# Values of the local attention projected in 64-column tiles onto both partition halves, copied by one ScalarE instruction in place of four

## The reference

```python
x = attn_layer(shift_tokens(x), Wqkv[i], q_scale[i], k_scale[i], Wo[i]) + x
x = ffn_layer(shift_tokens(x), ln_g[i], ln_b[i], W1[i], b1[i], W2[i], b2[i]) + x
```

## Time and profile before

| | |
|---|---|
| three timed runs | 2869.66, 2869.91 and 2871.89 us, median 2869.91 |
| profiled execution, span on the core | 2876.8 us |
| busy: PE / DVE / ACT / POOL | 2397.0 / 2534.2 / 1993.5 / 1164.0 us |
| value projection, PE L412 | 384 matmul records (two for each instruction), mean 623 ns |
| value copy, ACT L587 | 768 instructions, mean 375 ns, 287.6 us |
| granted TensorE clock, mean | 0.934 of full speed |

### The profile page before, as it was taken

How to read it: one execution, slowest core, us unless ns; L and a number is a source line. 1 busy time by engine, 2 the same in 40 slices (tenths; PEclk the granted TensorE clock), 3 DMA queues, 4 the chain that set the end, 5 groups by cost and what they waited for, 6 DMA issues and landing times. The chain is left out here.

```text
span 2876.8 us, 60131 instructions
## 1 busy us (share of the span) xinstructions
PE 2397.0 (83%) x23276; PEld 1231.6 (43%) x23276; DVE 2534.2 (88%) x2784; ACT 1993.5 (69%) x3169; POOL 1164.0 (40%) x465
## 2 busy tenths in 40 slices
PE   7788898888988889898898888988898765556778
PEld 2344444444444444444444444444444322222256
DVE  5799999899999999999999999999998499999642
ACT  4777787777877778777787777877787563343433
POOL 0344444343444434444444444434443046566220
PEclk8899999999999999999999999999999877777889
DMA  0100000000000000000000000000000100000001
GB/s 26 43 2 2 2 23 9 9 2 2 23 9 9 2 2 23 9 9 2 2 23 9 10 2 2 23 9 10 2 1 1 34 0 0 0 0 0 16 15 44
DMA packets 16015, 29.82 MB, mean 10 GB/s; under 512 B 3616, under 2 KB 6064, under 8 KB 15664
## 3 DMA queue, kind: packets, MB, share of 16 engines
q1 hardware_dynamic: 15760, 25.78, 2.9%
HBM read 24.73 MB, written 1.05 MB: 9 GB/s over the span
## 5 line engine op out<-in xcount | busy, mean ns | idle before, releaser
L697 POOL TENSOR_TENSOR f_rot<-f_raw,f_tabc 128x1024 f32<-128x1024 f32 x192 | 453.2, 2361 | 1070.6 <-DVE f_qk L745 576.5
L701 POOL TENSOR_TENSOR f_rot<-f_rot,f_shuf 128x1024 f32<-128x1024 f32 x192 | 451.5, 2351 | 235.7 <-DVE f_shuf L738 235.7
L738 DVE TENSOR_TENSOR f_shuf<-f_shuf,f_tabs 128x1024 f32<-128x1024 f32 x192 | 420.6, 2191 | 8.7
L596 ACT ACTIVATE f_raw<-f_ps 128x1024 f32<-128x1024 f32 x192 | 196.2, 1022 | 315.6 <-PE f_ps L423 315.6
L770 DVE TENSOR_TENSOR f_s<-f_s,f_rcp 128x512 f32<-128x512 f32 x192 | 400.6, 2087 | 6.6
L422 PE MATMUL f_ps<-f_xs,f_wq 128*128 128x512 f32 x384 | 229.2, 681 | 133.8 <-ACT f_rn L605 95.0
L464 PEld LDWEIGHTS f_ps<-f_ptz,f_v 64*64 64x64 f32 x6144 | 259.9, 133 | 152.3 <-issue 152.3
L1125 POOL TENSOR_TENSOR s_prod<-s_state,s_cs 128x1024 f32<-128x1024 f32 x64 | 234.1, 3676 | 167.3 <-DVE s_state L1203 137.0
L960 PE MATMUL s_ps<-s_prod,s_ident 128*128 128x512 f32 x256 | 182.9, 873 | 133.8 <-POOL s_prod L1125 133.6
L587 ACT ACTIVATE f_v<-f_ps 64x256 f32<-64x256 f32 x768 | 287.6, 375 | 6.6
L464 PE MATMUL f_ps<-f_ptz,f_v 64*64 64x96 f32 (+1 forms) x6144 | 286.2, 243 | 2.2 <-ACT f_ptz L617 2.2
(11 more groups left out here) (263 smaller groups left out, 4035.6 us busy)
## 6 DMA issues: line engine op xcount, KB each, us to landing
e_w<-in_e_w SPq DMA_DIRECT2D x16, 256.0 KB, 2.8
f_wq<-in_f_wq SPq DMA_DIRECT2D x12, 256.0 KB, 2.7
f_wk<-in_f_wk SPq DMA_DIRECT2D x12, 256.0 KB, 3.5
f_wv<-in_f_wv SPq DMA_DIRECT2D x12, 256.0 KB, 3.6
f_wo<-in_f_wo SPq DMA_DIRECT2D x6, 512.0 KB, 3.2
f_w<-in_f_w SPq DMA_DIRECT2D x6, 341.0 KB, 3.0
s_dx<-in_k_pick SPq DMA_DIRECT2D x1, 1536.0 KB, 8.9
f_w<-in_f_w SPq DMA_DIRECT2D x6, 192.0 KB, 3.9
```

What stands on the lines that cost most here:

```text
L697: pool.tensor_tensor(view(rot, 0, [S, 4], [1, S]), view(raw, 0, [S, 4], [1, S]), view(tab_c, 0, [S, 2], [0, 2], [1, S]), ALU.mult).then_in ...
L701: pool.tensor_tensor(rot[:, :], rot[:, :], shuf[:, :], ALU.add).then_inc(sem["rot"], 1)
L738: dve.tensor_tensor(view(shuf, 0, [S, 4], [1, S]), view(shuf, 0, [S, 4], [1, S]), view(tab_s, 0, [S, 2], [0, 2], [1, S]), ALU.mult).then_i ...
```

## The change

`values` computes the same numbers with four products in place of one. Each has 64 tokens (r = 0 or 1) as stationary operand, hence 64 columns of the array, and 256 columns of the weights (four heads of parity h, taken as four runs of 64) as moving operand. Its result lands on partitions 64h to 64h+63, columns 256r to 256r+255 of the bank. The semaphore is raised by the last one. `value_copy` is then a single instruction over 128 partitions and 512 elements. Waits and their places stay the same, and so do all other instructions.

```diff
-                pe.matmul(bank(2), xs[:, 128 * (q % 4):128 * (q % 4) + 128], wv[:, CH * (q // 4):CH * (q // 4) + CH],
-                          start=True, stop=True).then_inc(sem["v_mm"], 1)
+                for r in range(2):
+                    for h in range(2):
+                        at = 128 * (q % 4) + 64 * r
+                        mm = pe.matmul(view(ps, 2 * CH + 256 * r, [1, 256], p0=64 * h, rows=64), xs[:, at:at + 64],
+                                       view(wv, CH * (q // 4) + 64 * h, [128, 4], [1, 64]),
+                                       start=(r == 0), stop=True, skip_group_check=True)
+                mm.then_inc(sem["v_mm"], 1)
...
-                for r in range(2):
-                    for h in range(2):
-                        ins = act.activation(view(v, (2 * (q % 4) + r) * CH + 256 * (q // 4), [64, 4], [1, 64], p0=64 * h, rows=64),
-                                             view(ps, 2 * CH + 64 * h, [128, 4], [1, 64], p0=64 * r, rows=64), ACT.Copy)
-                ins.then_inc(sem["v"], 1)
+                act.activation(view(v, 2 * (q % 4) * CH + 256 * (q // 4), [CH, 2], [1, 256]),
+                               view(ps, 2 * CH, [256, 2], [1, 256]), ACT.Copy).then_inc(sem["v"], 1)
```

## The result

| | before | after |
|---|---|---|
| median of the runs on one chip | 2869.78 us (2868.29 to 2871.89, 4 runs) | 2792.55 us (2791.31 to 2795.49, 4 runs) |
| ratio | 1 | 0.9728, 95% interval 0.9714 to 0.9742 |
| profiled execution, span | 2876.8 us | 2793.7 us |
| busy PE / DVE / ACT / POOL | 2397.0 / 2534.2 / 1993.5 / 1164.0 us | 2381.0 / 2538.0 / 1806.5 / 1165.2 us |
| granted clock, mean | 0.934 | 0.947 |

A forecast was written before the change was run, and what follows sets the result against it. DVE was taken as the bound most of the time, so only its 97 us of waits could be gained. 8.4 us from 21 units plus 6.6 from the clock gave 15: 2854.9 us from the median, range 2842 to 2882.

The forecast's parts named there:

- The issue wait behind the jump: 2.73 us in which slot 0's scores wait for issue only; claimed to move along with its length unchanged.
- the lead of slot 6: Shorter value copy in slot 6 lets PE's projection of slot 7 go earlier: gain 0.70 us per unit.
- The ceiling of 97 us: DVE's idle waits, 69.7 us for the raw copy and 27.7 us for the scores, cap any gain.
- ACT's part: One 0.60 us copy replaces four taking 1.53 us in 192 slots: 179 us less busy, useful only in slot 6.
- 0.70 us from the chain through slots 6 and 7: PE's L422 of slot 7 goes at 1149.04 instead of 1149.74, cutting DVE's wait in slot 0 by 0.7 us.
- the net of 0.40: Per unit, 0.70 us gained less 0.30 lost in slots 0 and 1; over 21 units 8.4 us.
- Full overlap of the halves: In `values`, products on the array's two column halves run beside each other: 0.86 us, as now.
- Both rivals of longer `values`: Half overlap: 0.21 us lag per `values`, 2884 us, chance 0.10. No overlap: 0.85 us more per slot, 2935 us, 0.08.
- The tile change, 0.15 us per `values`: Switching PE to tiles before `values` costs 0.09 us plus an estimated 0.05 for the first weight load.
- The clock: PE's half-speed stretch behind the issue wait is long in five of 21 units; three fewer would save 6.6 us.
- The rival "more": Free changes between tile kinds (14.7 us) and no long half-speed stretch left (11 us): 2844 us, chance 0.10.

The follow-up runs named there:

- b_pad120: Kernel before plus 120 idle PE instructions in three places (119 by the trace), putting the loop head about where the change puts it: 2799.74 us, ratio 0.9757.
- a_pad136: Changed kernel plus 136 idle PE instructions (135 by the trace), returning the loop head to within one instruction of its old place in a block: 2887.05 us, ratio 1.0058.
- a_four: Changed kernel with its new products, but four copies of 64 partitions and 256 elements again in place of the single copy: 2794.76 us, ratio 0.9714.
- b_one: Kernel before with its old products, but the single copy of 128 partitions and 512 elements (values land in wrong places): 2875.96 us, ratio 0.9997.
- b_late: Kernel before with DVE's last product of slot 7, for which L511 waits, placed behind the normalisation: 2899.44 us, ratio 1.0103.
- b_pad131: Kernel before plus 131 idle semaphore increments at the start of PE's program, block end 135 behind the loop head: 2846.36 us, ratio 0.989.

## Why the prediction was wrong

The step that failed: "The issue wait behind the jump moves along: its length doesn't change by anything here, though the loop body gets 5% more PE instructions". I had the right wait and the right cause for it to change in one sentence, and dismissed it. The wait was not the jump's: it stood inside `scores`, after three records, and its length hung on where a 16 KB block of instructions ends. The change, through 120 more instructions ahead of the loop, removed it: 0.74 us of issue wait in place of 2.73, a difference above the 0.3 us that I had named as the sign of being wrong. Taking it away was worth 4.0 us per unit, 84 us. The same shift but for one instruction, without the change, gives the same time per unit (b_pad120), and the change without the shift gives nothing (a_pad136). That the kernel got faster, as forecast, was luck: of the forecast's two terms, the lead of slot 6 brought nothing, and the clock's came as part of another mechanism.

Step by step:

- *The ceiling of 97 us* held: 87 us of these waits went, and the loop got 84 us shorter, DVE's busy time being 4 us longer. No kernel that left DVE's work as it was gained more.
- *ACT's part* held: 192 copies of 0.58 us (0.60 predicted), ACT's busy time down by 187 us (179 predicted). That it is worth nothing in most slots is shown by a_four.
- *0.70 us from the chain through slots 6 and 7* did appear on PE and did not reach the next unit. The jump starts from DVE's product, which does not move, because DVE runs without a gap from slot 2 to there. b_one had PE's lead and none of the tile changes, and its ratio is 0.9997 (0.9987 to 1.0007), so the 0.70 was about 0 (0.2 at most, by the units with a short stretch at half speed), and the net of 0.40 with it. That I let the lead run through L511, because it "waits for DVE's product, about 0.7 us before it now", overlooked that the branch behind it does not queue with the matmuls: it follows the product by 0.16 us (b_late).
- *Full overlap of the halves* held: eight records of L415 and the change to L469 take 1.02 us (1121.02 to 1122.04) where 0.95 stood before and 1.06 was expected. Both rivals of longer `values` are refuted.
- *The tile change, 0.15 us per `values`*: from the end of the projection ahead to the product behind, 0.95 + 1.02 = 1.97 us after (1120.07 to 1122.04), against 0.86 + 0.95 = 1.81 before; 0.16. It costs nothing, since PE has slack beside DVE.
- *The clock*: I expected three of the five long half-clock stretches to go, for 6.6 us, as a matter of slip. All five went, and 15 of the 16 short ones, with the stop. The price was a little high: by the trace's times from branch to branch a unit with a long stretch takes 91.06 us and one with a short one 89.16, so 1.9 us and not 2.2. How much of the 4.0 us per unit was the stop and how much the clock behind it no run separates; b_pad131, which kept a stop (mean 1.90 us) and a short stretch behind 14 jumps, kept half of the time.
- *The rival "more"* had the right sign of error and the wrong mechanism; its 2844 us and the low end of 2842 lie 50 us above what came, because no case had a term for the issue wait.

What is left for the change itself: at the good layout 2792.55 and 2793.37 us (ratios 0.9728 and 0.9739, intervals overlapping), no difference; with b_pad120, whose block end lies one instruction from that of after, 85.60 us per unit against 85.64. At the bad one a_pad136's median lies 17.8 us above that of before (2887.05 and 2869.26), of which 7.0 are pads at the start (first shuffle at 95.4 for 88.4); the loops of the two profiled executions differ by 2.9 us (2119.7 and 2116.8). The rest, 8 us, is about the 6.9 us by which the profiled execution of before was longer than its median, and stays open.

## What to carry to other kernels

In a kernel with a hardware loop, look at the records right behind the jump: if a run of like instructions is split by an issue wait with an instruction transfer beside it, the code's position costs time, and a few idle instructions ahead of the loop may give it back. Compare two versions of such a kernel only at the same position of the loop's head within a block, or a change gets credit for a shift. And carry a lead on an engine over a jump only if the event behind which the branch comes moves too. A change that frees an engine which isn't the bound can be worth nothing as it stands and 30 us once work is moved onto it.

## What was not expected of the hardware

- PE's code is brought in packets of 16384 bytes; shifting it by 120 + 135 = 255 instructions brings the same stop back, one instruction later (4 records ahead of it in place of 3).
- Behind a jump the first scores start about 4.0 us after the branch, and a block end within the next two dozen instructions adds 2.5 to 2.7 us of standstill (means of the five kernels; single jumps 2.2 to 3.3); one 135 behind the head adds 1.90 (1.5 to 2.4); at 146, 147 and 240 none above 0.3 us is seen.
- A semaphore increment on PE takes about 0.15 us where PE has nothing else to do; 131 of them, 0.15 us apart in b_pad131, moved the first shuffle by 13.7 us (to 102.1), while 26 beside other work moved nothing (87.1).
- Products on 128 rows by 64 columns run beside each other in float32: eight records of 256 columns in 1.02 us, though their loads share all rows.
